# Third layer's attention: keys and values once for all heads, head weights multiplied beforehand, slots in another order

## What is computed

```python
q = z @ wq @ fcq_w + fcq_b        # z: [b, 256, 128], wq: [128, 64], fcq_w: [64, 16*64]
k = z @ wk @ fck_w + fck_b
v = z @ wv @ fcv_w + fcv_b
scores = einsum('bihd,bjhd->bhij', q, k) / sqrt(64)
attn = softmax(scores, axis=-1)
out = einsum('bhij,bjhd->bihd', attn, v).reshape(b, n, 16*64) @ fco_w + fco_b
```

## Time and profile before

| | us |
|---|---|
| median of 3 runs | 2787.68 (2783.92 to 2794.81) |
| profiled execution, span | 2860.1 |
| layer 2 in it, first centring matmul to end of its last residual | 1284.4 to 2139.4 |
| TensorE / VectorE / ScalarE / GpSimd busy, share of the span | 89% / 64% / 46% / 43% |

### The profile page before, as it was taken

How to read it: one execution, slowest core, us unless ns; L and a number is a source line. 1 busy time by engine, 2 the same in 40 slices (tenths; PEclk the granted TensorE clock), 3 DMA queues, 4 the chain that set the end, 5 groups by cost and what they waited for, 6 DMA issues and landing times.

```text
span 2860.1 us, 39521 instructions
## 1 busy us (share of the span) xinstructions
PE 2550.0 (89%) x13960; PEld 1617.9 (57%) x13960; DVE 1839.4 (64%) x3692; ACT 1323.6 (46%) x3393; POOL 1239.4 (43%) x1120
## 2 busy tenths in 40 slices
PE   6787799999999999979879999999999689897988
PEld 3475355555555555554445666666555358676766
DVE  5777467776776777656756777777665644656623
ACT  4575524434344243334445666665456224455433
POOL 2553267777677676743552333331000721233331
PEclk8799899999999999979999999999999778889888
DMA  4463200000000000009311222222101342212113
GB/s 167 141 204 111 99 1 1 1 1 1 1 1 1 1 1 1 1 4 241 92 38 53 68 67 68 67 64 57 30 1 46 90 133 48 55 42 57 40 40 96
DMA packets 186516, 159.27 MB, mean 56 GB/s; under 512 B 98336, under 2 KB 165344, under 8 KB 185504
## 3 DMA queue, kind: packets, MB, share of 16 engines
q1 hardware_dynamic: 163536, 90.70, 11.6%
q0 software_dynamic: 22784, 66.05, 7.4%
HBM read 126.94 MB, written 59.51 MB: 65 GB/s over the span
## 4 chain that ended last, share of the span: by engine, by line
PE 43%; DVE 5%; ACT 3%; issue 3%; another core or an unknown queue 1%; POOL 0%; DVEq 0%; ACTq 0%
PE bank L65 38%; PE bank L2099 4%; ACT L3298 1%; DVE work L2055 1%; DVE work L3360 0%; ACT weights_odd L3024 0%; DVE work L3412 0%; PE bank L2971 0%; DVE work L2032 0%; DVE work L3563 0%; PE bank L672 0%; DVE work L2107 0%; PE bank L3108 0%; DVE work L3528 0%
## 5 line engine op out<-in xcount | busy, mean ns | idle before, releaser
L1535 POOL TENSOR_TENSOR work<-work 128x512 f32<-128x512 f32 x384 | 488.7, 1273 | 299.9 <-DVE work L1527 280.1
L65 PE MATMUL bank<-work 64*128 64x256 f32 (+5 forms) x4384 | 593.7, 354 | 23.2 <-DVE work L3563 7.2
L65 PE MATMUL bank<-weights_odd,normed_channels 128*128 128x512 f32 (+2 forms) x1088 | 509.3, 575 | 53.1 <-DVE work L1527 52.6
L65 PEld LDWEIGHTS bank<-work 64*128 64x128 f32 (+4 forms) x4384 | 415.5, 172 | 225.5 <-issue 152.9
L1527 DVE TENSOR_TENSOR work<-bank,work 128x512 f32<-128x512 f32 x360 | 244.6, 687 | 112.7 <-PE bank L65 101.4
L2069 ACT ACTIVATE work<-bank,work 128x256 f32<-128x256 f32 x512 | 235.6, 472 | 159.9 <-DVE work L2055 153.2
L65 PEld LDWEIGHTS bank<-weights_odd,normed_channels 128*128 128x128 f32 x1088 | 176.1, 193 | 180.0 <-DVE work L1527 99.3
L2055 DVE TENSOR_REDUCE work<-bank 128x2 f32<-128x512 f32 x256 | 165.4, 686 | 173.5 <-PE bank L65 150.6
L599 POOL DMA_INDIRECT weights_even<-in_L_Wx,expert_slots x112 | 111.7, 998 | 339.9 <-PE bank L672 271.6
L1602 ACT ACTIVATE work<-bank,work 128x256 f32<-128x256 f32 x256 | 118.8, 469 | 295.4 <-DVE work L1589 295.1
L65 PE MATMUL bank<-work,weights_odd 128*128 128x512 f32 (+2 forms) x520 | 199.3, 505 | 25.0 <-ACT work L3323 9.0
(11 more groups left out here) (345 smaller groups left out, 4472.4 us busy)
## 6 DMA issues: line engine op xcount, KB each, us to landing
...
```

Of the source, the lines that this page charges most:

```text
L65: return pe.matmul(out, lhsT, rhs, start=first, stop=last, skip_group_check=True)
L1535: gp.tensor_tensor(self.sum_of(p), self.sum_of(p), self.product_of(p), ALU.add).then_inc(s["l1_add"], 1)
```

## The change

Keys and values are no longer made per head. Since a head's score is `(z wq fcq + b)(z wk fck + b)^T`, the head's `fck` is multiplied into the query weights beforehand: `Fq = wq @ fcq_h @ fck_h^T`, and every head scores against the same 64 numbers `z wk`. In the same way every head multiplies its probabilities with the same 64 numbers `z wv`, and `fcv_h @ fco_h` is multiplied beforehand into the output weights `Fvo`. The biases go into a query bias, into the output bias and into a number per token and head (`shift`), which is constant along a row of scores; `vector_bias` subtracts it from the negated maxima and adds it again, in two tiny VectorE instructions per unit. All four exponentials of a unit now wait for these.

`tensor_joint` makes the products from 78 small matmuls in four parts. `tensor_z` makes for each group, in the norm's loop, one array with the logits, the shift and the shared values (four matmuls of 88 columns) and the shared keys (one of 512 columns); VectorE copies both to SBUF (`vector_z`). In the slots the value matmuls and the key matmuls are gone, and the query matmul stays, in even slots.

TensorE's slot now runs: transposes of half 0, value product, scores, transposes of half 1, query, fold, experts. ScalarE copies the transposed half 1 before the exponentials instead of behind them. VectorE copies half 0 directly behind the inverses.

```diff
@@ class Layer2, __init__ and load @@
-        self.Fk = work.take(2 * GW)
-        self.v = [work.ring(2) for _ in range(TPG)]
-        self.q, self.kk = work.ring(2), work.ring(2)
+        self.zk, self.z = work.take(TOKENS), work.take(TILES * L2_Z).rearrange("p (t w) -> p t w", w=L2_Z)
+        self.q = work.ring(2)
...
     def tensor_joint(self, pe, on):
         s, b = self.k.sem, self.k.bank[4:8]
+        halves = [slice(half * L2_DH, (half + 1) * L2_DH) for half in range(2)]
         on.wait_ge(s["l2_small"], self.SMALL)
+        for m in range(L2_PAIRS):
+            for r in halves:
+                last = mm(pe, b[0][r, m * L2_DH:(m + 1) * L2_DH], self.FqT[r, m, :], self.FkT[r, m, :])
+        last.then_inc(s["l2_joint_mm"], 1)
+        for m in range(L2_PAIRS):
+            for r in halves:
+                mm(pe, b[1][r, m:m + 1], self.FkT[r, m, :], self.q_b[r, m:m + 1])
+                mm(pe, b[1][r, L2_PAIRS + m:L2_PAIRS + m + 1], self.FqT[r, m, :], self.k_b[r, m:m + 1])
+        for m in range(L2_PAIRS):
+            last = mm(pe, b[1][:, 2 * L2_PAIRS:2 * L2_PAIRS + 1], self.Fo[:, m, :], self.v_b[:, m:m + 1], first=m == 0, last=m == L2_PAIRS - 1)
+        last.then_inc(s["l2_joint_mm"], 1)
+        yield
+        for m in range(L2_PAIRS):
+            for r in halves:
+                last = mm(pe, b[2 + m // 4][r, m % 4 * P:(m % 4 + 1) * P], self.FvT[r, m, :], self.Fo[r, m, :])
+        last.then_inc(s["l2_joint_mm"], 1)
+        yield
+        on.wait_ge(s["l2_joint"], 4)
+        for half, r in enumerate(halves):
+            last = mm(pe, b[half][:, :], self.Wq[r, :], self.joint[r, :])
+        last.then_inc(s["l2_joint_mm"], 1)
+        yield
+        on.wait_ge(s["l2_joint"], 6)
+        for half, r in enumerate(halves):
+            mm(pe, b[2 + half][:, 0:L2_PAIRS], self.Wq[r, :], self.to_bias[r, :])
+            last = mm(pe, b[2 + half][:, L2_PAIRS:2 * L2_PAIRS], self.k.ones[r, :], self.both_b[r, :])
+        last.then_inc(s["l2_joint_mm"], 1)
+        yield
     def vector_joint(self, v, on):
...
+            v.tensor_copy(self.Fvo[:, 4 * i:4 * (i + 1), :], tiles(b[2 + i][:, :])).then_inc(done, 1)
+            v.tensor_copy(self.Wz[:, EXPERTS:EXPERTS + L2_HEADS][:, c], b[2 + half][:, 0:L2_PAIRS]).then_inc(done, 1)
...
+    def tensor_z(self, pe, on, g):
+        on.wait_ge(s["l2_joint"], self.JOINT)
+        on.wait_ge(s["ln_done"], GROUPS * self.n + g + 1)
+        on.wait_ge(s["l2_z"], 2 * (g - 1))
+        for i in range(TPG):
+            t = TPG * g + i
+            last = mm(pe, self.b_z[g % 2][:, i * L2_Z:(i + 1) * L2_Z], k.xn[:, t * P:(t + 1) * P], self.Wz)
+        last.then_inc(s["l2_z_mm"], 1)
+        mm(pe, self.b_keys[g % 2][:, :], self.Wk, cols(k.xn, g)).then_inc(s["l2_z_mm"], 1)
+    def vector_z(self, v, on, g):
+        s = self.k.sem
+        on.wait_ge(s["l2_z_mm"], 2 * g + 1)
+        v.tensor_copy(self.z[:, TPG * g:TPG * (g + 1), :], self.b_z[g % 2][:, 0:TPG * L2_Z].rearrange("p (t w) -> p t w", w=L2_Z)).then_inc(
+            s["l2_z"] if g < GROUPS - 1 else s["logits"], 1)
+        on.wait_ge(s["l2_z_mm"], 2 * g + 2)
+        v.tensor_copy(cols(self.zk, g), self.b_keys[g % 2][:, :]).then_inc(s["l2_z"], 1)
+    def vector_ahead(self, v, on):
+        yield from self.vector_joint(v, on)
+        for g in range(GROUPS):
+            self.vector_z(v, on, g)
+            yield
+    def vector_shift(self, v, on):
+        s = self.k.sem
+        on.wait_ge(s["logits"], self.router.nth + 1)
+        to = self.z[:, :, EXPERTS:EXPERTS + L2_HEADS]
+        v.tensor_tensor(to, to, self.shift.unsqueeze(1).to_broadcast([P, TILES, L2_HEADS]), ALU.add).then_inc(s["l2_shifted"], 1)
+    Z = 2 * GROUPS - 1
...
+    def query_pair(slot):
+        return n if half == 0 and 0 <= n < L2_PAIRS * GROUPS else None
+    def tensor_query(self, pe, on, n):
+        s, (g, m) = self.k.sem, divmod(n, L2_PAIRS)
+        on.wait_ge(s["l2_q"], n)
+        mm(pe, self.b_misc[:, :], self.Fq[:, m * P:(m + 1) * P], cols(self.k.xn, g)).then_inc(s["l2_q_mm"], 1)
+    def vector_query(self, v, on, n):
+        s, m = self.k.sem, n % L2_PAIRS
+        on.wait_ge(s["l2_q_mm"], n + 1)
+        on.wait_ge(s["l2_score"], 4 * (n - 1))
+        v.tensor_scalar(self.q[n % 2], self.b_misc[:, :], self.q_bias[:, m:m + 1], L2_DH ** -0.5, ALU.add, ALU.mult).then_inc(s["l2_q"], 1)
@@ tensor_score @@
-        on.wait_ge(s["l2_qk"], 2 * pair + 2)
+        on.wait_ge(s["l2_q"], pair + 1)
         on.wait_ge(s["l2_exp"], 2 * (h - 2))
-        q, kk = self.q[pair % 2][r, t], self.kk[pair % 2][r, t]
+        q, kk = self.q[pair % 2][r, t], cols(self.zk, g)[r, t]
@@ vector_max and vector_bias @@
-        on.wait_ge(s["l2_exp"], 2 * (h - 7))
-        v.tensor_reduce(self.mx[h % 8][:, 0:2], self.b_score[h % 3][:, :].rearrange("p (i j) -> p i j", j=SEQ), AX.X,
+        on.wait_ge(s["l2_exp"], 4 * (n - 3))
+        v.tensor_reduce(self.mx[n % 4][:, 2 * half:2 * half + 2], self.b_score[h % 3][:, :].rearrange("p (i j) -> p i j", j=SEQ), AX.X,
                         ALU.max, negate=True).then_inc(s["l2_max"], 1)
+    def vector_bias(self, v, on, n):
+        s, (g, m, b) = self.k.sem, self.unit(n)
+        t = TPG * g + TPG // BPG * b
+        shift = self.z[:, t:t + 2, EXPERTS:EXPERTS + L2_HEADS].rearrange("p t (e m) -> p e t m", e=2)[:, :, :, m]
+        mx = self.mx[n % 4][:, 0:4].rearrange("p (e t) -> p e t", e=2)
+        on.wait_ge(s["l2_shifted"], 1)
+        on.wait_ge(s["l2_max"], 2 * n + 2)
+        v.tensor_tensor(mx, mx, shift, ALU.subtract).then_inc(s["l2_bias"], 1)
+        on.wait_ge(s["l2_bias"], 2 * n + 1)
+        v.tensor_tensor(mx, mx, shift, ALU.add).then_inc(s["l2_bias"], 1)
@@ scalar_exp @@
-        on.wait_ge(s["l2_max"], h + 1)
+        on.wait_ge(s["l2_bias"], 2 * n + 2)
@@ tensor_times_v, tensor_fold @@
-        on.wait_ge(s["l2_v"], 8 * g + 4 * (m // 4) + 4)
-                last = mm(pe, self.b_o[r:r + L2_DH, b * SEQ:(b + 1) * SEQ], self.v[2 * b + jc][h // 8][:, c],
+                last = mm(pe, self.b_o[r:r + L2_DH, b * SEQ:(b + 1) * SEQ], self.z[:, TPG * g + TPG // BPG * b + jc, EXPERTS + L2_HEADS:],
-        mm(pe, self.b_fo[:, :], self.Fo[:, m, :], self.o[pair % 2], first=m == 0, last=m == L2_PAIRS - 1).then_inc(s["l2_fold"], 1)
+        mm(pe, self.b_fo[:, :], self.Fvo[:, m, :], self.o[pair % 2], first=m == 0, last=m == L2_PAIRS - 1).then_inc(s["l2_fold"], 1)
@@ slot loops: tensor, scalar, vector @@
         for slot in range(self.FIRST, self.LAST):
             for which, at in enumerate(self.COUNTS):
                 if slot == at:
                     known, mask = ((18, r.first), (self.FIRST_READ, r.second))[which]
                     self.moe.tensor_count(pe, on, which, mask, self.b_moe, r.at + known)
-            if (n := self.due(slot, 0)) is not None:
-                self.tensor_score(pe, on, n, 0)
-                self.tensor_score(pe, on, n, 1)
-            self.tensor_shared(pe, on, slot, ("v",))
             if (n := self.due(slot, 2)) is not None:
                 self.tensor_turn(pe, on, n, 0)
             if (n := self.due(slot, 3)) is not None:
                 self.tensor_times_v(pe, on, n)
-            self.tensor_shared(pe, on, slot, ("qk",))
+            if (n := self.due(slot, 0)) is not None:
+                self.tensor_score(pe, on, n, 0)
+                self.tensor_score(pe, on, n, 1)
             if (n := self.due(slot, 2)) is not None:
                 self.tensor_turn(pe, on, n, 1)
+            if (n := self.query_pair(slot)) is not None:
+                self.tensor_query(pe, on, n)
...
+            if (n := self.due(slot, 2)) is not None:
+                self.scalar_turned(a, on, n)
             if (n := self.due(slot, 0)) is not None:
                 self.scalar_exp(a, on, n, 0)
                 self.scalar_exp(a, on, n, 1)
-            if (n := self.due(slot, 2)) is not None:
-                self.scalar_turned(a, on, n)
...
-        self.norm.vector(v, on, self.vector_joint(v, on))
+        self.norm.vector(v, on, self.vector_ahead(v, on))
+        self.vector_shift(v, on)
         route = self.vector_route(v, on)
         for _ in range(4):
             next(route)
         for slot in range(self.FIRST, self.LAST):
             if (n := self.due(slot, 1)) is not None:
                 self.vector_inverse(v, on, n)
-                if n >= self.BY_GPSIMD:
-                    self.normalise(v, on, n, 0)
+            if (n := self.due(slot, 2)) is not None:
+                self.vector_turned(v, on, n)
+            if (n := self.due(slot, 1)) is not None and n >= self.BY_GPSIMD:
+                self.normalise(v, on, n, 0)
             if (n := self.due(slot, 0)) is not None:
                 self.vector_max(v, on, n, 0)
                 self.vector_max(v, on, n, 1)
-            self.vector_shared(v, on, slot, ("v",))
-            if (n := self.due(slot, 2)) is not None:
-                self.vector_turned(v, on, n)
+                self.vector_bias(v, on, n)
```

(5 more changed lines are left out.)

165 lines of the change are left out of this document (63 added, 102 removed).

## The result

The changed kernel takes 2799.5 us (median of 20 runs) where the kernel before takes 2783.6 (20 runs), a ratio of 1.006 (1.0045 to 1.0074): **16 us slower**. The forecast was 25 slower, 2758 to 2845.

A forecast was written before the change was run, and what follows sets the result against it. TensorE was taken to bound slots 32 to 104, and chains through three engines afterwards. Terms 26 + 4 + 10 - 20 + 5 + 0.5 gave +25.5, scaled to +25 on 2787.7: 2812 us, range 2758 to 2845.

The forecast's parts named there:

- Chain B: Even to odd slot: first maximum, exponentials, ScalarE's copy of a pair's outputs, value product, scores, next maximum; 6.53 us.
- chain A: Back to VectorE: first maximum, exponentials, inverse, copy of half 0, scaling, next maximum; 5.0 us per slot.
- The start: Layer 2 up to its first maximum, with the joint products and each group's `tensor_z`: +26 us, bounds +12 and +38.
- Part one of the joint: First small matmuls of `tensor_joint`, 96 records of 64x64 and 16 of 128x128: 14 us at half clock, +11.
- Slots 12 to 32: Layer 2 slots without expert matmuls, while GpSimd scatters: +10 us, bounds 0 and +22.
- With the same 41: Slots 12 to 32: 41 us of waits in all engines stay, added to 115 us from the two chains.
- Slots 0 to 12, 104 to 127, the tail: Layer 2's first slots, last slots and what follows the last unit: +4, +5 and +0.5 us.
- The nine plain ones: Slots 104 to 107 and 122 to 126: from a mean of 4.4 us to 5.76 each, +12 us.
- slots 32 to 104: Layer 2 slots with experts: two slots take 11.5 us, 415 us in all, -20 rather than TensorE's own -70.
- a cheap start: Rival: small matmuls at the start run at full clock and overlap; start +12, total +11, 2799 us; chance 0.18.
- The output copy is never late: Rival: ScalarE's output copy finishes before TensorE's value product; slots 32 to 104 give -70, total 2734 us; chance 0.17.
- The clock fell: Rival: TensorE idling in the slots lowers its clock; plain 40 slots cost +60, 2850 us and more; chance 0.12.

## Why the prediction came out as it did

*Chain B* was right in kind and nearly so in size: 6.36 and 4.90 for 6.53 and 5.0. The step that was 0.17 off is from the first exponential to the output copy, 1.81 measured for 1.98. I had added the durations of rows, 0.21 for the last sum's reading among them, and 0.05; but the next row starts 0.12 before that one ends (1709.97 and 0.21, then 1710.06). The 4.90 is 0.10 under chain A's 5.0, mostly between the inverse and the copy, 0.09 where I had the 0.22 to the scaling. Over 36 pairs the two make 10 us, and in 72 slots the term was -27.3, not -20. The bias from maximum to exponential was 1.71 for 1.72.

*The start* was the worst term, +26 for +13.6. Part one of the joint took 5.9 us, where I had 14. TensorE, from the first small matmul on, by the clock of the pieces: in the first are the 64x64 records, in the second one-column records over 64 rows, in the third one-column records over the array; last, the whole of part one in the slow profile of the same kernel.

```profile
1282.20:1284.10 1.90, 1.90 (x38) 1.87 (x39) 0.00 (x0) 0.60 (x1) 0.00 (x0) 0.54 0.45 61
1284.10:1286.10 2.00, 2.00 (x68) 1.99 (x65) 0.69 (x1) 0.00 (x0) 0.00 (x0) 1.00 0.79 227
1286.10:1288.10 2.00, 2.00 (x16) 2.00 (x17) 0.00 (x0) 0.00 (x0) 0.00 (x0) 0.81 0.79 254
```
```profile
1288.10:1296.80 8.70, 8.70 (x114) 8.68 (x113) 0.69 (x1) 0.60 (x1) 0.00 (x0) 0.50 0.87 273
```

Two steps were wrong. The first is the price: with the clock at 0.50 all through, part one took 8.7 us, not 14. There a record over 64 rows costs 0.055 whether it has 64 columns or one, and a one-column record over the array 0.21. The second is the clock, half throughout in my sum: it rose to 1.00 in the second piece, where the one-column records over 64 rows took 0.03 each, and was 0.81 in the third; that gave the other 2.8 us. The clock is not the same in every run of this code: the start took 55.5 us in the two quick profiles and 58.1 in the slow one, and 58.1 in another kernel's profile from the quick chip (the new arithmetic in the old order), so it is not the chip.

So part one was 3.2 more than the products it replaces, not 11. Parts two to four, the wait for the last copies (2.5 for 3.0) and the norm's matmuls at half clock came to 6.7 more, for 10; from there to the first maximum it was 3.7 for +5. The Trainium skill's rule (TensorE: Matmul & The Clock Gate, section "Why this matters for your kernels"), that matmuls on different quarters run at once, had been left out of the sum. By it and my own prices part one at half clock would be 5.4 + 3.8 = 9.2, and 8.7 agrees (the term would then be +16, not the +17 that I wrote). It is not shown: the products of the earlier trace rows alternate between the two halves too (`tensor_sum`), and they cost the same 0.056 at a granted clock of 1.00, so that another limit, the same in both, may be what the 0.055 shows. No run puts such products on one half alone.

*Slots 12 to 32* hold two errors that depend on the chip. "With the same 41" was the failed step: those waits go with the chip of the trace, and the times with another. On the quick chip there are none in the changed kernel's profile, and the chains cost some +20, not +10, as worked out above. On the slow one the waits stayed, and the change cost nothing: -3 to -10 against the three profiles of before, under the lower bound of 0.

*Slots 0 to 12, 104 to 127, the tail*: +4.2, +3.0 and +2.1 for +4, +5 and +0.5. In the slots with joins TensorE stayed the bound, as forecast: 8.19 where they mostly took 9.29 and 10.15, 10.7 less over the eight for the 10 of the sum. The nine plain ones had taken 4.6 on average, not the 4.4 that I read from one pair (the 3.76 is the last slot's alone), which made that term 2 too dear.

The terms on the quick chip are 13.6 + 4.2 + 20 - 27.3 + 3.0 + 2.1 = +16, but the 20 was itself worked out from the 16, so this sum tests nothing. The forecast of +25 came out 9 too high: the start was 12 too dear and slots 32 to 104 7 too dear, slots 12 to 32 some 10 too cheap. The mechanism of slots 32 to 104 was right; that the total came so near is partly luck. Of the rivals, "a cheap start" was right in kind: +13.6 for its +12, with a clock that rose. Its total, 2799, is the measured one, and that is luck too, since it kept the same +10 and -20. "The output copy is never late" did not happen, but is one instruction's place away: with the copy moved ahead it did, 0.975 beside 0.998 on slow chips. The clock fell a little in the plain slots (0.96 in 104 to 127 after 0.99, 0.88 in 0 to 12 after 0.97) and was 1.00 in 32 to 104, where TensorE idled 11% of the time.
